# Head 0's exponentials before the routing chunk's sigmoid in ScalarE's order

## The reference, cut to what matters

```python
c  = bi_wkv(x, f, f, w, u, cond)             # sigmoid(x) * (num / den), from two scans of f
q, k, v = c @ Wq + bq, c @ Wk + bk, c @ Wv + bv
p  = softmax(q @ k.T * scale + causal_mask)  # 16 heads
x1 = x + (p @ v) @ Wo + bo
c2 = bi_wkv(x1, f, f, w2, u2, cond)          # = sigmoid(x1) * f2
scores = sigmoid(c2 @ gate_w)                # 32 experts in 4 groups, 2 groups kept, 6 experts chosen
out = x1 + sum_of_chosen_experts(c2) + shared_expert(c2)
```

## Time and profile before

| what | value |
|---|---|
| median of 3 runs | 2279.98 us (2278.03 to 2283.61) |
| the profiled execution | 2272.61 us |
| its span, first to last instruction | 2270.9 us |
| mean granted TensorE clock | 0.977 |
| TensorE busy | 2141.2 us, 94% |
| VectorE busy | 1357.4 us, 60% |
| ScalarE busy | 1160.4 us, 51% |
| GpSimd busy | 1431.8 us, 63% |

### The profile page before, as it was taken

How to read it: one execution, slowest core, us unless ns; L and a number is a source line. 1 busy time by engine, 2 the same in 40 slices (tenths; PEclk the granted TensorE clock), 3 DMA queues, 4 the chain that set the end, 5 groups by cost and what they waited for, 6 DMA issues and landing times. The chain is left out here.

```text
span 2270.9 us, 39956 instructions
## 1 busy us (share of the span) xinstructions
PE 2141.2 (94%) x11247; PEld 1860.2 (82%) x11247; DVE 1357.4 (60%) x2501; ACT 1160.4 (51%) x2491; POOL 1431.8 (63%) x953
## 2 busy tenths in 40 slices
PE   3999999999999999989899989999999999999996
PEld 2788888888878878777777879889999999998875
DVE  8778888888856686666765533333333333333386
ACT  5587777777767777767663123333333333333310
POOL 8787778778755666666672321466586868653365
PEclk9899999999999999989998999999999999999998
DMA  5633445443365546665345553566666676664666
GB/s 135 182 101 122 134 132 169 156 135 102 113 226 167 158 151 192 210 208 168 123 133 199 205 166 108 159 182 191 179 194 201 194 203 189 201 192 128 178 208 203
DMA packets 367657, 380.29 MB, mean 167 GB/s; under 512 B 51556, under 2 KB 283560, under 8 KB 362728
## 3 DMA queue, kind: packets, MB, share of 16 engines
q1 hardware_dynamic: 256520, 252.46, 36.1%
q10 hardware_dynamic: 95584, 75.01, 10.7%
q0 software_dynamic: 15360, 50.34, 6.8%
HBM read 264.21 MB, written 120.59 MB: 169 GB/s over the span
## 5 line engine op out<-in xcount | busy, mean ns | idle before, releaser
L2113 POOL TENSOR_SCALAR we_high<-we_raw 128x1408 fp32r<-128x1408 f32 (+1 forms) x94 | 132.1, 1405 | 304.8 <-PE up_e L708 232.0
L2115 POOL TENSOR_TENSOR we_low<-we_raw,we_high 128x1408 fp32r<-128x1408 f32 (+1 forms) x94 | 312.1, 3321 | 7.8
L2328 DVE TENSOR_TENSOR hidden_e<-silu_e,up_e 128x352 f32<-128x352 f32 x127 | 66.2, 521 | 250.3 <-ACT silu_e L2267 250.3
L2311 DVE TENSOR_TENSOR hT_low<-hT_ps,hT_high 128x256 fp32r<-128x256 f32 x127 | 53.9, 425 | 252.8 <-ACT hT_high L2253 252.8
L2267 ACT ACTIVATE silu_e<-gate_e 128x352 f32<-128x352 f32 x127 | 59.0, 465 | 284.0 <-PE up_e L708 272.1
L708 PE MATMUL gate_e<-we_high,xT_high 128*128 x508 | 176.2, 347 | 11.3 <-DVE xT_low L2318 6.4
L2272 ACT ACTIVATE rows_out<-down_e 128x512 f32<-128x512 f32 x127 | 75.9, 598 | 197.4 <-PE down_e L708 197.2
L708 PE MATMUL gate_e<-we_high,xT_low 128*128 x508 | 164.5, 324 | 0.0
L708 PE MATMUL up_e<-we_high,xT_high 128*128 x508 | 164.1, 323 | 0.0
L708 PE MATMUL gate_e<-we_low,xT_high 128*128 x508 | 164.0, 323 | 0.0
L708 PE MATMUL up_e<-we_high,xT_low 128*128 x508 | 163.6, 322 | 0.0
(11 more groups left out here) (403 smaller groups left out, 7197.4 us busy)
## 6 DMA issues: line engine op xcount, KB each, us to landing
slots_out<-rows_out ACTq DMA_DIRECT2D x127, 256.0 KB, 2.4
rows_early<-slots_in ACTq DMA_DIRECT2D x500, 64.0 KB
we_raw<-L_ffn_w_gate SPq DMA_DIRECT2D x32, 704.0 KB, 4.8
we_raw<-L_ffn_w_up SPq DMA_DIRECT2D x32, 704.0 KB, 5.0
w_ring<-L_attn_Wq SPq DMA_DIRECT2D x64, 256.0 KB, 3.1
q_T<-q_out SPq DMA_DIRECT2D x64, 256.0 KB, 2.5
w_ring<-L_attn_Wk SPq DMA_DIRECT2D x64, 256.0 KB, 3.5
w_ring<-L_attn_Wv SPq DMA_DIRECT2D x64, 256.0 KB, 3.7
```

What stands on the lines that cost most here:

```text
L2113: nc.gpsimd.tensor_scalar(wh[:, p, at:to], raw[:, at:to], 1.0, 1.0, ALU.mult, ALU.mult).then_inc(w_hi, 1)
L2115: nc.gpsimd.tensor_tensor(wl[:, p, at:to], raw[:, at:to], wh[:, p, at:to].bitcast(F32), ALU.subtract).then_inc(w_split, 1)
L2328: nc.vector.tensor_tensor(hb[:], sg[:], psu[:], ALU.mult).then_inc(h_done, 1)
```

## The change

In ScalarE's second list (iterations 8 to 11) the token `E0` moves ahead of `mS0`. Every other token and every other list stays.

```diff
 ACT_ORDER = (
...
-    "u u mG mS0 E0 mH0 u u V0 V1 N0 E1 V2 r2 V3 hk a0 mR0 u r3 Q0 u u he N1 b0 K2 mS1 a1 u Q1 u A0 mH1 K3 E2 u b1 Q2 u N2 mR1 A1 a2 E3 b2 N3 Q3 u u a3 A2 b3 u k0 k1 u A3 h0 u h1".split(),
+    "u u mG E0 mS0 mH0 u u V0 V1 N0 E1 V2 r2 V3 hk a0 mR0 u r3 Q0 u u he N1 b0 K2 mS1 a1 u Q1 u A0 mH1 K3 E2 u b1 Q2 u N2 mR1 A1 a2 E3 b2 N3 Q3 u u a3 A2 b3 u k0 k1 u A3 h0 u h1".split(),
```

## The result

Over 20 runs each, the changed kernel has a median of 2289.16 us (2279.2 to 2303.41) and the kernel before 2282.47 us (2278.03 to 2288.2); the ratio is 1.0028, with a 95% interval of 1.0016 to 1.0040. On 2282.47 us that is 6.4 us slower, from 3.7 to 9.1. I had forecast +0.7 us and a range of 2275.5 to 2285.5, up to 5.5 us above the 2279.98 of the first three runs; 2289.16 lies outside. Part of that distance is the level: over 20 runs the kernel before has 2282.47 us, 2.5 more than over the first three. The side came out as forecast, but that was not worth much: a sum of +0.7, with a range of its own from -1.5 to +2.5, hadn't decided it. The 0.93 for "the same" (within 0.3%) came out too, though over 20 runs each the interval of the ratio does tell the change from none. The size was wrong.

A forecast was written before the change was run, and what follows sets the result against it. TensorE, with almost no room, was taken as the bound in iterations 8 to 11; shifts of -2.0, +1.4, +2.7 and -1.4 us summed to +0.7, giving 2280.7 us on the median's level, range 2275.5 to 2285.5.

The forecast's parts named there:

- only TensorE's gaps count: Iterations 8 to 11: TensorE busy 268.5 of 281 us, so only its idle time and new waits count.
- Iterations 8, 9 and 11: Shift of the row transposes T0: 2.0 us gained in 8, 1.4 lost in 9, 1.4 gained in 11.
- 1.43 us for mX0: ScalarE's mH0, now waiting for VectorE's multiplication mX0, starts 1.43 us after the chunk's sigmoid does.
- the load before E1: ScalarE needs a new exponentials' table load behind N0, so E1 starts 3.2 us after N0.
- 1.48 us from V0 to V2: TensorE's third value projection V2 starts 1.48 us after ScalarE's V0.
- Iteration 10, the term that failed: Two loads more, and 2.92 us from mX0 to i0 on VectorE; T0 at 806.0 against 803.36, 2.7 us lost.
- a wait of 2.2 us before V2 in iteration 10: New TensorE wait in iteration 10, about 2.2 us: V2 at 798.4 against 796.2.
- If each answer from VectorE costs 0.3 us: Bound for iterations 8 to 11: answers to ScalarE at 0.3 us instead of 0.07 make the sum +1.6 us.
- Gains given back: Rival: a late DMA landing cancels the gains of iterations 8 and 11, losses remain; +4.1 us, 2284.1; chance 0.23.
- the losses swallowed: Rival: losses of iterations 9 and 10 don't reach T0, only gains stay; -3.4 us, 2276.6; chance 0.17.
- no effect: Rival: only handed-on waits move, T0 stays where it is in all four iterations; 2280.0 us; chance 0.10.
- about +10 us: Sum by the skill page's 2.66 us per table switch, two switches in each chain dearer by 1.3 us.

The follow-up runs named there:

- the kernel with 8 and 11 alone: Kernel before with E0 ahead of mS0 in iterations 8 and 11 only; ratio 0.9990 (0.9972 to 1.0009).

## Why the prediction was wrong

- **What bounds the kernel, and that only TensorE's gaps count:** right, but for the clock. T0's shift carried through to the next S0 in each of the four iterations: from T0 to S0 lie 52.2, 52.2, 56.7 and 52.2 us in the first profiles of both kernels.
- **Iterations 8, 9 and 11:** -2.05, +1.36 and -1.47 us against -2.0, +1.4 and -1.4. The steps (1.43 us for mX0, the load before E1, 1.48 us from V0 to V2) hold to 0.1 us. In a second pair of profiles iteration 11 gave +1.3, as before's chunk was earlier there; the forecast took one landing time for a fixed one.
- **Iteration 10, the term that failed.** The step was: "From mX0 to head 0's reciprocal i0 are 2.92 us (789.91 to 792.83)", taken over from the row of before and so "**2.7 us lost**". The change moved mX0 and the choice behind it to where GpSimd makes the splits that ScalarE's two `u` release. It took 5.01 us there. From S0 to T0, iteration 10 took 16.38 us before, 23.08 changed, 20.2 with the splits later. So of 6.7 us, 3.8 are order and tables with a short fall of the clock (V2 to V3 4.31 instead of 2.84, 1.5 us, of which about 1.1 appear at T0 beyond my 2.7), and 2.9 are GpSimd's: 2.1 us of waiting, the rest a clock that stays low longer (5.22 us). With mG beside mS0 as well and the clock up, S0 to T0 took 17.92 us: 1.5 of the 6.7 remain, as in iteration 9.
- **The clock.** I had read it as 1.00 over the stretch and gave it no price. I forecast a wait of 2.2 us before V2 in iteration 10 and didn't ask what TensorE does after such a gap. Behind gaps of 1.86 to 4.02 us before V2 in iteration 10 it ran at the 1.2 GHz level in all six profiles that have one; behind 0.86 us and less it did not. The length of the gap alone doesn't decide: the 2.58 us before V2 in iteration 8, in the second profile of the changed kernel, left the clock at 1.00. Elsewhere before V2 it fell behind 3.74 and 3.84 us (iteration 11, with mH0 behind V1) and stayed up behind 1.65 to 1.75. What does decide is open. Behind the old gaps of 2.8 us later in iteration 10, and behind those of iteration 8, it fell in some profiles and not in others.
- **Bounds.** "If each answer from VectorE costs 0.3 us" was the only upper bound on that engine. It was drawn from VectorE's latency and left out who works beside it.
- **Rivals.** Gains given back did not happen (iteration 9 of the kernel with 8 and 11 alone has 68.57 us). Nor were the losses swallowed, nor was there no effect: T0 moved in all four iterations. The Trainium skill's rule on grouping calls by table set (ScalarE: Activation LUTs, Table sets: the hidden batching unit) holds in direction: with the group kept, 0.6 to 0.7 us less at T0, for a load of 1.28 us. The drain that the same page of the Trainium skill counts (What ACT_TABLE_LOAD costs) is not seen here either: in the changed kernel the exponential starts 1.29 us after its load starts (660.26 to 661.55). The "about +10 us" by that figure was overdrawn besides: it counted two bare switches in each of the four chains, where the order before has one already; by my own chains the change adds 0, 1, 2 and 1 of them, which with that page's figure would be an estimate of about +6 us.
- **What stays open.** The four iterations give +4.6 and +4.9 us, the runs +6.4 (+3.7 to +9.1). Whether the rest is more frequent falls of the clock further on can't be told from two profiles.

The Trainium skill has the rule that I missed: SBUF — State Buffer (Who interferes with whom) describes the port pair shared by VectorE and GpSimd as an exclusive lock held for the whole instruction, taken by VectorE's instructions with two SBUF inputs and by those in a two-port mode. The traces agree for iteration 10: the comparison, with two SBUF inputs, and the cast wait for GpSimd's end (1.27 and 1.24 us instead of 0.26 and 0.17), while the values' low parts, which read one input from PSUM, keep their 0.65 to 0.69 us in every profile, beside a GpSimd subtraction too. mX0, also with two SBUF inputs, ended behind GpSimd as well (6.19 us instead of 0.69), but as it began before the subtractions, the lock as described doesn't by itself say why it had to wait for all four.

## What to carry to other kernels

When an instruction is moved in one engine's order, look at what the other engines will be doing at its new time, not only at what it waits for: durations taken from the trace of before hold only with the same neighbours, and for VectorE that means GpSimd. A new gap on TensorE costs itself and, behind each of the six before V2 in iteration 10 (1.86 to 4.02 us), a stretch at half clock, 1.5 to 2.4 us more; one of 2.58 us in iteration 8 cost only itself. And an order shared by four iterations is four changes: here two gained, two lost, and a fact that held in one of them alone (the choice) decided the sum.

## What the runs showed of the hardware that I had not expected

- VectorE can stand beside GpSimd over several instructions: one multiplication took 6.19 us, until 0.55 us behind four back-to-back subtractions, and 6.09 us in another profile. Elsewhere VectorE got in between two of them.
- The price of a gap is not fixed, nor set by its length alone. The same gap of 2.8 us in iteration 10 was followed by full speed in one profile of before (73.08 us) and by a low clock in the other (74.70).
- ScalarE stood 7.62 and 17.16 us for "remote" in one execution, which was 12 us longer than all others in that part, one that no kernel here changes.
